# Order of work in the last two attention turns of a cross-attention and expert kernel

## The reference

```python
x = x + xattn(layernorm(x), ctx, Wq, bq, Wk, bk, Wv, bv, Wo, bo)   # 8 heads of 16, rotary q and k, softmax
x = x + ffn(layernorm(x), gate_w, w_gate_proj, w_up_proj, w_down_proj)

# ffn, on rows of 512 numbers (2048 rows in all), 32 experts, 8 of them per row
router_logits = x @ gate_w.T
sel_w, sel_e = top_k(router_logits, 8);  sel_w = softmax(sel_w)
out = sum over chosen e of  w_e * ((silu(x @ gate[e].T) * (x @ up[e].T)) @ down[e].T)
```

## Time and profile before

| what | value |
|---|---|
| median of 3 runs | 1092.52 us (1092.05 to 1094.72) |
| profiled execution | 1093.14 us, span from first to last instruction 1091.3 us |
| busy share PE / DVE / ACT / POOL | 92% / 64% / 71% / 68% |
| mean granted clock of PE | 0.966 of full |
| attention stage ends | last row store issued at 521.89 us, landed 2.12 us later |
| expert stage | from 528 us to the end |

### The profile page before, as it was taken

How to read it: one execution, slowest core, us unless ns; L and a number is a source line. 1 busy time by engine, 2 the same in 40 slices (tenths; PEclk the granted TensorE clock), 3 DMA queues, 4 the chain that set the end, 5 groups by cost and what they waited for, 6 DMA issues and landing times.

```text
span 1091.3 us, 29745 instructions
## 1 busy us (share of the span) xinstructions
PE 999.5 (92%) x7228; PEld 478.8 (44%) x7229; DVE 701.7 (64%) x1349; ACT 771.1 (71%) x1791; POOL 747.1 (68%) x675
## 2 busy tenths in 40 slices
PE   6689999999999999993499999999999999999995
PEld 2222222222222222231366666666666666666662
DVE  4778899999999988886354555453553554553521
ACT  2278888888888887781367667767677776677673
POOL 5434577777777774457467777777777777777774
PEclk9599999999999999996699999999999999999998
DMA  5524444444344333320588789898789898889673
GB/s 169 159 70 123 139 130 129 126 132 120 118 126 130 119 109 115 98 96 22 173 217 215 212 204 241 216 216 219 198 201 238 215 223 213 218 194 233 119 144 58
DMA packets 88948, 174.56 MB, mean 160 GB/s; under 512 B 23754, under 2 KB 40698, under 8 KB 84786
## 3 DMA queue, kind: packets, MB, share of 16 engines
q0 software_dynamic: 38144, 74.53, 32.0%
q1 hardware_dynamic: 50736, 99.26, 28.5%
q10 hardware_dynamic: 4, 0.02, 0.0%
HBM read 117.26 MB, written 61.58 MB: 164 GB/s over the span
## 4 chain that ended last, share of the span: by engine, by line
PE 41%; issue 4%; DVEq 3%; DVE 2%; DMA 1%; ACTq 1%; ACT 1%; POOL 1%; POOLq 0%; SPq 0%
PE ps L1873 22%; PE ps L1881 5%; PE ps L1899 2%; PE ps L1901 2%; PE ps L1903 2%; PE ps L1902 2%; PE ps L1900 2%; DVEq L374 2%; DVE w_lo L1463 1%; PE ps L1889 1%; DVE w_hi L1458 1%; PE ps L1891 1%; PE ps L1890 1%; ACTq L374 1%; POOL expert_rows L627 0%
## 5 line engine op out<-in xcount | busy, mean ns | idle before, releaser
L1086 DVE TENSOR_REDUCE mx<-ps 128x2 f32<-128x1024 f32 x256 | 303.9, 1222 | 33.9 <-PE ps L1845 29.9
L1873 PE MATMUL ps<-w_hi,o_raw 128*128 x1184 | 313.5, 327 | 0.0
L787 POOL DMA_INDIRECT out<-v,s_idx x148 | 248.2, 1677 | 94.1 <-ACT g_idx L803 41.5
L813 ACT ACTIVATE pr<-ps 128x512 f32<-128x512 f32 x512 | 278.6, 603 | 45.8 <-PE ps L1822 44.6
L766 POOL DMA_INDIRECT pr<-normalised_tokens,g_idx x150 | 163.0, 1087 | 51.8 <-issue 21.7
L1873 PE MATMUL ps<-w_lo,o_raw 128*128 x592 | 193.4, 327 | 0.0
L803 ACT ACTIVATE o_raw<-ps 128x1024 f16<-128x1024 f16 (+1 forms) x180 | 171.9, 955 | 1.3 <-PE ps L1881 1.1
L627 POOL DMA_INDIRECT expert_rows<-rows,rowi x128 | 129.1, 1008 | 38.3 <-issue 37.3
L1873 PEld LDWEIGHTS ps<-w_hi,o_raw 128*128 128x128 f16 x1184 | 116.1, 98 | 84.5 <-issue 0.7
L1475 DVE SCALAR_TENSOR_TENSOR rope_b<-rope_a,stacks,ps 128x192 f32<-128x192 f32 x148 | 60.6, 410 | 142.8 <-ACT rope_a L973 103.9
L1834 PE MATMUL ps<-pr,v 128*32 128x512 f32 x1024 | 136.4, 605 | 0.4 <-issue 0.3
(11 more groups left out here) (177 smaller groups left out, 1476.8 us busy)
## 6 DMA issues: line engine op xcount, KB each, us to landing
stage<-in_expert_w SPq DMA_DIRECT2D x32, 1280.0 KB
stacks<-qk_parts SPq DMA_DIRECT2D x128, 96.0 KB
w_lo<-in_x SPq DMA_DIRECT2D x32, 256.0 KB, 2.9
w_lo<-in_ctx SPq DMA_DIRECT2D x32, 256.0 KB, 5.7
qk_parts<-qk SPq DMA_DIRECT2D x32, 256.0 KB
qk_parts<-qk SPq DMA_DIRECT2D x32, 128.0 KB
out<-x SPq DMA_DIRECT2D x16, 256.0 KB, 4.8
normalised_tokens<-x2s SPq DMA_DIRECT2D x16, 256.0 KB, 2.5
```

What stands on the lines that cost most here:

```text
L787: nc.gpsimd.indirect_dma_start(out_rows, bass.IndirectOffsetOnAxis(s_idx[:, s.slot(4), 0:1], 0), y_sb[:, s.slot(4), :], None, bounds_check ...
L813: nc.scalar.activation(pr[:, n % 8, :], bank(f"s{n}"), ACT.Exp, scale=DH ** -0.5).then_inc(exp_done, 1)
L1086: V.tensor_reduce(mx[:, b.slot(2), at:at + 3:2, tile], bank(f"m{n}"), AXX, ALU.max).then_inc(mx_done, 1)
L1873: last = mm(ps[:, s.slot(2), 0:2 * INTER], xt[:, s.slot(2), at:at + P], w[:, cols], start=(m == 0), stop=(m == 3 * KT - 1))
```

## The change

Four orders of work change and nothing that is computed. On POOL, turn 16, the power for batch 15 comes behind one row store of batch 14 and not behind two. On DVE, turn 15, the weights of batch 13 come ahead of the residual of batch 14, and counts and places of batch 13 ahead of the normalisation of batch 14. On DVE, turn 16, counts and places of batch 14 come ahead of the product with the reciprocals of batch 15. On PE, turn 15, the counts product of batch 13 comes ahead of an average, `pv(4)`; in turn 16 that of batch 14 comes ahead of the spreading of the reciprocals.

```diff
--- before.py
+++ after.py
@@ -663,9 +663,9 @@
                     return
                 if turn_no == NB:
                     scatter_rows(bs, (0, 1, 2, 3, 4, 5, 6, 7))
-                    scatter_rows(br, (0, 1))
+                    scatter_rows(br, (0,))
                     inverse_deviation(bo)
-                    scatter_rows(br, (2, 3, 4, 5, 6, 7))
+                    scatter_rows(br, (1, 2, 3, 4, 5, 6, 7))
                     scatter_rows(bo, (0, 1, 2, 3, 4, 5, 6, 7))
                     return
                 if turn_no is not None and turn_no > NB:
@@ -1262,13 +1262,13 @@
                     first_weights_low(0, 5)
                     first_weights_low(1, 5)
                     link = choice(br)
+                    weights(br, link)
                     residual(bo)
                     stats_of_x2(bo)
                     variance_of_x2(bo)
-                    weights(br, link)
-                    normal_x2(bo)
                     read_counts(br)
                     places(br, link)
+                    normal_x2(bo)
                     low_of_x2(bo)
                     over_turned_sums(bo + 1, 0)
                     first_weights_low(2, 5)
@@ -1280,9 +1280,9 @@
                     link = choice(br)
                     over_turned_sums(bo, 1)
                     weights(br, link)
-                    times_reciprocals(bo, 1)
                     read_counts(br)
                     places(br, link)
+                    times_reciprocals(bo, 1)
                     residual(bo)
                     stats_of_x2(bo)
                     variance_of_x2(bo)
@@ -1666,8 +1666,8 @@
                     s(20)
                     output_of(bo, 1)
                     s(22)
+                    counts_of(br)
                     pv(4)
-                    counts_of(br)
                     s(24)
                     pv(5)
                     s(26)
@@ -1686,9 +1686,9 @@
                     sums_turned(bo, 1)
                     pe.wait_ge(x2_done, NB - 1)
                     output_of(bo, 0)
-                    reciprocals_spread(bo, 1)
                     pe.wait_ge(cnt_done, 2 * (NB - 2))
                     counts_of(br)
+                    reciprocals_spread(bo, 1)
                     output_of(bo, 1)
                     return
                 if turn_no == NB + 1:
```

## The result

| | before | after |
|---|---|---|
| median | 1092.9 us (19 runs, 1091.7 to 1097.8) | 1095.3 us (19 runs, 1093.7 to 1097.2) |
| span of the profiled execution | 1091.3 us | 1093.6 us |
| last row store issued | 521.89 | 523.82 |
| first gather | 527.98 | 530.06 |
| from there to the end of the span | 563.3 us | 563.5 us |

What follows compares the result with a forecast made beforehand. POOL's queue, through the last row store, was taken to bound the hand-over; one more store behind an earlier power put it at 521.03 against 521.89, 0.9 us faster, so median 1091.7 us, range 1089.8 to 1094.8.

Steps and rivals of the forecast that it cites:

- The last store sets the hand-over: From attention to expert steps, the last row store on POOL, issued at 521.89, moves the whole expert stage.
- the expert stage only shifts: Behind the hand-over, the expert stage starts from an idle PE either way and should only shift.
- Batch 13's 1.35 us: DVE, turn 15: places ahead of the normalisation make batch 13's indices ready at 486.91, 1.35 us sooner.
- the lateness of product and variance: DVE, turn 16: batch 15's product comes 1.6 us later, at 497.45, its variance 1.35 us later, at 501.46.
- POOL's wait before the power: POOL, turn 16: after batch 14's first store, 2.3 us of waiting for batch 15's variance, until 501.68.
- batch 13's gain would be waited away: POOL, turn 16: the whole 1.35 us that batch 13 gained is lost in the wait ahead of the power.
- the unexplained 2.11 us: POOL's idle gap ahead of batch 14's second store, with no known releaser; the sum let it vanish in POOL's wait.
- the 0.20 of the sum: POOL, turn 16: between the power's end at 502.25 and the next store at 502.45, only 0.20 us.
- rival A: POOL's gap stays and adds 2.11 us between power and second store: last store 522.94, slower by 1.05 us; chance 0.20.
- The 14 intervals behind it: POOL: from the store behind the power to the last store, 14 intervals of 18.58 us, where 13 took 17.31.
- the 0.8 us of excess: POOL: 13 store intervals hold 0.8 us over plain stores, put down to two-port VectorE instructions and kept in the sum.
- Its 520.2: POOL: last store at 520.2 if an order kept two-port VectorE instructions off the stores, 0.8 us more gain.

Runs made afterwards that it cites:

- two_extra: The changed kernel with two indirect stores more, both in turn 4, to a spare table: 1096.2 us in one run, against 1092.0 of the kernel before.
- four_left_out: The changed kernel without four of batch 2's eight row stores: 1092.6 us in one run, against 1092.0 of the kernel before.
- extra_stores: The changed kernel with 18 indirect stores more, three each in turns 4 to 9, to a table nothing reads: 1.0272 of the kernel before.
- extra_stores_turn15: The kernel before with turn 15's part of the change alone and 18 indirect stores more, three each in turns 4 to 9: 1.0266 of the kernel before.

## Why the prediction was wrong

I forecast 0.9 us faster and a median of 1091.7 in a range of 1089.8 to 1094.8; it is 2.3 us slower, at 1095.3.

**What held.** The last store sets the hand-over, and the expert stage only shifts (563.3 and 563.5 us). Batch 13's 1.35 us, the lateness of product and variance, and POOL's wait before the power all came within 0.5 us of the sum. That batch 13's gain would be waited away held as well: batch 14's first store came 1.76 us sooner and the power's wait took 2.45.

**The step that failed** is "In this sum the unexplained 2.11 us disappears behind POOL's wait". The wait hid nothing. POOL's idle starts only once the power is out of the way, and is 2.81 us there against the 0.20 of the sum: 2.61 us of the miss. Before, the same idle stood between the two stores, while batch 15's variance was on its way, and the power found its variance ready. The change put the wait for the variance ahead of it, and now both are paid, one behind the other. That was rival A, to which I gave 0.20: its mechanism is what happened, and its price of 1.05 us was too low against the 1.93 of the last store, mostly because it took 2.11 us for an idle that is 2.81 behind a power. The evidence that I weighed against the rival ruled out only the x2 store as its cause, not that the idle would follow the second store.

**The term that was too small.** The 14 intervals behind it took 19.03 us (504.79 to 523.82) and not 18.58, 0.45 more. The normalisation no longer meets a store (502.01 falls in the idle), but one store takes 1.56 us beside DVE's step plan (513.71, beside L1415 from 513.48), and the last three now meet DVE's split of the expert weights, which starts at 521.12 (523.66 before) since batch 15's chain ends sooner; they take 1.45, 1.14 and 1.12 us. The Trainium skill (SBUF — State Buffer, "SBUF: two separate sides") states that a VectorE instruction in a two-port mode keeps GpSimd from writing descriptors until it ends. The trace agrees for the store at 520.62: it ends at 522.07, 0.12 us behind the split's first instruction (521.95).

The other longer stores run beside DVE instructions that read two tensors in SBUF (L1415, L1463), and no run shows what lengthened them. That bears on the prediction too: of the 0.8 us of excess that it put down to two-port instructions, 0.33 is the store beside the normalisation, and the rest is nearly all in stores of 1.11 to 1.13 us (508.76, 510.19, 516.67) beside L1160, L1188 and L1417, which read two tensors as well. Its 520.2 for an order without such meetings is not shown. The miss adds up: -0.27 for the earlier power, +2.61, +0.45 are 2.79 us, and 523.82 less 521.03 is 2.79.

**What the parts were worth.** With the gap away, the change had 22.7 to 22.8 us from batch 14's first store to the last (two_extra, four_left_out), as the sum said. But the old order has 22.1 with the gap inside. That suggests that the power behind one store would not be the better order even without the gap, since the old place, behind two stores, filled POOL's time until the variance was there. It is not shown. In the one pair without the gap on one chip, extra_stores has 24.19 us and extra_stores_turn15, with turn 16 as before, 21.96, but there batch 14's first store comes 2.0 us later behind batch 13's, so that from batch 13's first store to the last it is 42.01 against 41.81, and the times are equal (1.0272 and 1.0266).

**Open.** What the idle of 2 to 3 us is. It comes once, ahead of batch 14's second store; it stays with 40 instructions more ahead, 40 behind, 3 late, with the pads in 6, 12 or 22 pieces and with four stores made direct; it leaves with two or 18 indirect stores more or four fewer. No count of instructions, transfers or descriptors that I tried fits all of these. The records of the two DMA queues that the profile calls "instruction" show no packet in the idle, before (500.72 to 502.83) or after (501.98 to 504.79), which speaks against a load of code but does not rule it out. A kernel with turn 15's part, turn 16 as before and no gap should beat both, by the readings above; it was run only with the 18 stores that remove the gap and cost more than it, so this is not shown. Why signals from PE come late on chips 2, 3 and 4 with turn 15's order is open too.

## What to carry to other kernels

An idle that nothing recorded explains is a cost with a place of its own: until a run has moved it, count it in full and behind any wait that a change puts ahead of it. Before a wait is moved forward in a queue, ask what the engine did in that time so far; here it was a stall that now comes after. And a gain ahead of a wait is worth nothing until the wait's own chain is shorter: 1.76 us of earlier stores ended in 2.45 us of waiting.

## What was not expected of the hardware

POOL's idle of 2.81 us behind a power, the same to 0.01 us in ten traces (nine kernels), and of 2.1 to 2.2 us behind a store; that two indirect stores more, twelve turns earlier, move it by 16 transfers and four fewer make it go. And that one order can be worth 0.9994 on one chip (with three semaphore increments more) and 1.0041 and 1.0045 on others, where the read of PE's transposes comes 4.2 us late.
